# Gate logits with the tokens stationary, affinity transposes moved into the next image, and two weight splits moved to GpSimd

## The reference

```
x = x + attention(layernorm_c(x))          # 8 heads of 64, softmax over 1024 keys, fp32
t = tokens(x)
n = layernorm(t)
logits   = n @ gate_weight                 # 512 x 16 experts
affinity = softmax(logits).T               # [image, expert, token]
gating, index = top_k(affinity, 128)       # per image and expert
h = gelu(n[index] @ w1[e] + b1[e]);  y = h @ w2[e] + b2[e]
t = t + scatter_add(index, gating * y)
```

## Time and profile before

| what | value |
| --- | --- |
| median of three runs | 3219.74 us |
| profiled execution, its own time | 3216.83 us |
| span of the profiled execution | 3215.0 us |
| mean granted TensorE clock | 0.984 |
| PE busy | 3059.6 us (95%) |
| DVE busy | 2278.2 us (71%) |
| ACT busy | 1850.1 us (58%) |
| POOL busy | 1093.1 us (34%) |

### The profile page before, as it was taken

The page is one execution under the profiler, slowest core; times in us unless marked ns, Lnnn a source line. Parts: engine busy times, 40 slices in busy tenths (PEclk is TensorE's granted clock), DMA queues, the critical chain, the costliest instruction groups (busy, mean ns, idle before and its releaser), DMA issues. The chain is left out here.

```text
span 3215.0 us, 49747 instructions
## 1 busy us (share of the span) xinstructions
PE 3059.6 (95%) x18114; PEld 2627.4 (82%) x18114; DVE 2278.2 (71%) x3481; ACT 1850.1 (58%) x3353; POOL 1093.1 (34%) x1112
## 2 busy tenths in 40 slices
PE   6999999999999999999999999999917999999998
PEld 5988889888888888887988889888816788888886
DVE  5887688688768877876888688587775655655653
ACT  4876678477657857774876678477612333333332
POOL 1225224322512351252225124322513444444443
PEclk9999999999999999999999999999968999999999
DMA  7122121321321132113123121311224666666564
GB/s 236 37 60 106 64 63 50 112 67 37 105 88 50 50 115 77 37 57 118 58 60 109 61 63 57 105 41 37 63 96 94 135 141 133 135 143 137 129 144 59
DMA packets 121438, 283.59 MB, mean 88 GB/s; under 512 B 22417, under 2 KB 30609, under 8 KB 110481
## 3 DMA queue, kind: packets, MB, share of 16 engines
q1 hardware_dynamic: 92560, 213.72, 20.1%
q0 software_dynamic: 28672, 67.13, 11.8%
HBM read 173.08 MB, written 74.15 MB: 77 GB/s over the span
## 5 line engine op out<-in xcount | busy, mean ns | idle before, releaser
L754 DVE TENSOR_TENSOR PT<-ring,PT 128x512 fp32r<-128x512 f32 x1024 | 676.5, 686 | 160.4 <-ACT PT L503 142.2
L503 ACT ACTIVATE PT<-ring 128x512 fp32r<-128x512 f32 x1024 | 582.7, 597 | 169.8 <-PE ring L876 87.2
L908 PE MATMUL O<-PT,V 128*128 128x256 f32 x4096 | 673.0, 289 | 0.0
L696 DVE TENSOR_REDUCE nmax<-S 128x1 f32<-128x1024 f32 x512 | 619.8, 1211 | 71.7 <-PE S L865 71.7
L876 PE MATMUL ring<-ident,prob 128*128 128x128 f32 x4096 | 614.1, 273 | 15.3 <-DVE PT L754 12.9
L908 PEld LDWEIGHTS O<-PT,V 128*128 128x128 f32 x4096 | 575.4, 189 | 40.2
L865 PE MATMUL S<-kd,qs 128*128 128x512 f32 x2048 | 599.0, 414 | 2.7 <-ACT prob L494 1.7
L494 ACT ACTIVATE prob<-S,nmax 128x1024 f32<-128x1024 f32 x512 | 571.3, 1116 | 36.4 <-DVE nmax L696 36.4
L432 POOL COPY oS<-oHL 64x256 f32<-64x256 f32 x256 | 100.9, 394 | 1282.3 <-ACT oHL L552 1276.3
L876 PEld LDWEIGHTS ring<-ident,prob 128*128 128x128 f32 x4096 | 463.9, 139 | 55.3 <-issue 49.5
L865 PEld LDWEIGHTS S<-kd,qs 128*128 128x128 f32 x2048 | 347.2, 189 | 50.5 <-issue 6.0
(11 more groups left out here) (115 smaller groups left out, 3457.7 us busy)
## 6 DMA issues: line engine op xcount, KB each, us to landing
kd<-kd SPq DMA_DIRECT2D x128, 256.0 KB, 3.6
wraw<-w_dram SPq DMA_DIRECT2D x32, 1024.0 KB, 7.3
wqk<-wqk_split SPq DMA_DIRECT2D x24, 1024.0 KB, 4.8
xt<-x_dram SPq DMA_DIRECT2D x16, 1024.0 KB, 7.5
Rs<-rinv_rows SPq DMA_DIRECT2D x56, 256.0 KB, 3.4
PT<-wv_split SPq DMA_DIRECT2D x7, 2048.0 KB, 8.9
oT<-x_dram SPq DMA_DIRECT2D x24, 512.0 KB, 3.3
out_dram<-oT SPq DMA_DIRECT2D x48, 256.0 KB, 8.3
```

The lines of the kernel that those rows point to most:

```text
L503: nc.scalar.activation(PT[:, 0, u // 2 % 2, 4 * c:4 * c + 4, u % 2 * P:u % 2 * P + P], ring[:, k % 2, :].rearrange("p (m q) -> p m q", m=4 ...
L696: nc.vector.tensor_reduce(nmax[:, s:s + 1], S[:, s % 2, :], AX.X, ALU.max, negate=True).then_inc(max_done, 1)
L754: nc.vector.tensor_tensor(PT[:, 1, here[0], here[1], here[2]], ring[:, k % 2, :].rearrange("p (m q) -> p m q", m=4), PT[:, 0, here[0], her ...
L908: last_mm = nc.tensor.matmul(O[:, m % 2, 0:QC], V[:, t, head // 2, 2 * (head % 2):2 * (head % 2) + 2, :].rearrange("p h d -> p (h d)"), PT ...
```

## The change

It has two parts: the gate stage, and the start of the kernel.

Gate stage (PE, ACT and DVE lists):

```
# PE: the product, tokens stationary; one signal behind the eighth tile
-  last_mm = products(O[0:E, i // 4, i % 4 * P:i % 4 * P + P],
-                     [(gate_sb[:, c, :], n2T[:, i % 2, c, :]) for c in range(KC)])
-  if i % 4 == 3:
+  last_mm = products(O[:, 0, i * E:(i + 1) * E],
+                     [(n2T[:, i % 2, c, :], gate_sb[:, c, :]) for c in range(KC)])
+  if i == NT - 1:
       last_mm.then_inc(logits, 1)
# PE: the eight logit transposes and their wait go
-  pe.wait_ge(logits_copied, b * 2 + 2)
-  ... eight nc.tensor.transpose(O[:, 0, i * E:(i + 1) * E], affT[...], ident[0:E, 0:E])
# PE: affinity transposes, from ahead of scores(3) to between the halves of unit 1
+  def turn_affinities(j):
+      pe.wait_ge(soft, j * 5 + 5)
+      for h in range(2):
+          for i in range(4):
+              last_t = nc.tensor.transpose(O[0:E, 1 - h, i * P:(i + 1) * P], aff[:, 4 * h + i, :], ident)
+          last_t.then_inc(affT_filled, 1)
   # in turn_and_multiply
   turn_probs(b, u, c)
+  if u == 1 and c == 0 and b > 0:
+      turn_affinities(b - 1)
   # in product_with_v, part 0 of m == 0
+  if b > 0:
+      pe.wait_ge(affT_copied, b * 2)
# ACT: copy_logits (two activations an image) goes; the affinity copies move
   high_of_probs(b, s - 2)
+  if s == 3 and b > 0:
+      copy_affinities(b - 1)
# DVE: gate maximum and difference ahead of maximum(1), the rest behind it
   maximum(b + 1, 0)
-  maximum(b + 1, 1)
-  dve.wait_ge(logits_turned, b + 1)
+  dve.wait_ge(logits, b + 1)
   ... gmax, lg ...
+  if not last:
+      maximum(b + 1, 1)
   dve.wait_ge(soft_exp, b + 1)
   ... gsum, grec, aff ...
```

Start (POOL, ACT, DVE, SP lists):

```
# POOL, ahead of the low parts of V: the low parts of the V weights (0) and of split 2
+  for w in (0, 2):
+      pool.wait_ge(w_hi, w + 1)
+      raw, hi, lo, _ = splits[w]
+      nc.gpsimd.tensor_tensor(lo, raw, hi.bitcast(F32), ALU.subtract).then_inc(w_lo[w], 1)
# DVE keeps splits 1 and 3
-  if i in (3, 5, 7):
-      low_of_weights((i - 3) // 2)
+  if i == 5:
+      low_of_weights(1)
# ACT: the wait for the Q and K weights moves behind the second tile; casts behind tiles 1 and 2
-  act.wait_ge(wqk_raw_in, 32)
   for i in range(NT):
       high_of_norm(0, i)
-      if i in (1, 3):
-          high_of_weights(1 + i // 2)
+      if i in (1, 2):
+          act.wait_ge(wqk_raw_in, 32)
+          high_of_weights(i)
# ACT: the projected K waits for the K stage's stores alone, Q for the rest
-  act.wait_ge(w_out, 16 * 4 * (PAIRS - 1))
-  high_of_proj(0, 0)
+  act.wait_ge(w_out[0], 16 * 2 * (PAIRS - 1))
+  high_of_proj(0, 0, 0, 2)
+  act.wait_ge(w_out[1], 16 * (PAIRS - 1))
+  high_of_proj(0, 0, 2, 4)
# SP: each split is stored as soon as it is there; the load of Wo stands behind the first pair's stores
+  for j in range(2):
+      sp.wait_ge(w_lo[1 + j], 1)
+      for h in range(2):
+          store_split(0, j, h, w0_out)
   ... load Wo, wait w0_out, load_first_pair() ...
+  for j, h, n in ((0, 0, 0), (0, 1, 0), (1, 0, 1), (1, 1, 2)):
+      for p in range(1, PAIRS):
+          store_split(p, j, h, w_out[n])
```

More of the change, by code:

```diff
@@ L166, in attention @@
         w_hi = sem("w_hi")
-        w_lo = sem("w_lo")
+        w_lo = [sem(f"w_lo{w}") for w in range(4)]
         wv_out = sem("wv_out")
         w0_out = sem("w0_out")
-        w_out = sem("w_out")
+        w_out = [sem(f"w_out{i}") for i in range(3)]
         consts_in = sem("consts_in")
@@ L302, in _, with store_split @@
                 sp.dma_start(raw, wT[j]).then_inc(wqk_raw_in, 16)
-            sp.wait_ge(w_lo, 1)
+            sp.wait_ge(w_lo[0], 1)
             sp.dma_start(wv_dram, wv.bitcast(F32)).then_inc(wv_out, 16)
[L305 to L317, removed]
+            def store_split(p, j, h, done):
+                half = staged(j, h).bitcast(F32).rearrange("p (k c) -> p k c", k=KC)
+                sp.dma_start(wqk_dram[p, :, 2 * j + h, :, :], half[:, :, p * P:(p + 1) * P]).then_inc(done, 16)
+            for j in range(2):
+                sp.wait_ge(w_lo[1 + j], 1)
+                for h in range(2):
+                    store_split(0, j, h, w0_out)
+            raw = oT[:, 0:2, :].rearrange("p a n -> p (a n)").rearrange("p (k c) -> p k c", k=KC)
+            sp.dma_start(raw, wT[3]).then_inc(wo_raw_in, 16)
+            sp.wait_ge(w0_out, 16 * 4)
+            load_first_pair()
+            for j, h, n in ((0, 0, 0), (0, 1, 0), (1, 0, 1), (1, 1, 2)):
+                for p in range(1, PAIRS):
+                    store_split(p, j, h, w_out[n])
+            sp.wait_ge(w_out[2], 16 * (PAIRS - 1))
+            sp.wait_ge(w_out[1], 16 * (PAIRS - 1))
+            sp.wait_ge(w_out[0], 16 * 2 * (PAIRS - 1))
             load_pair(1)
@@ L510, in high_of_weights, with copy_affinities @@
                 nc.scalar.activation(hi, raw, ACT.Copy, scale=scale).then_inc(w_hi, 1)
+            def copy_affinities(j):
+                for i in range(2):
+                    act.wait_ge(affT_filled, j * 2 + i + 1)
+                    nc.scalar.activation(affT[:, 512 * i:512 * i + 512], O[0:E, 1 - i, :], ACT.Copy
+                                         ).then_inc(affT_copied, 1)
             act.wait_ge(ones_set, 1)
@@ L585, in image @@
                     high_of_proj(b + 1, 0, 0, 3)
[L587 to L590, removed]
                 for i in range(NT):
@@ L609, in image @@
                     high_of_probs(b + 1, 0)
[L610 to L613, removed]
+                if last:
+                    copy_affinities(b)
             all_images(act, image)
@@ L882, in _ @@
                 if i == 3:
-                    pe.wait_ge(w_lo, 1)
+                    pe.wait_ge(w_lo[0], 1)
                 if i >= 3:
@@ L893, in _ @@
             scores(0, 2)
-            pe.wait_ge(w_lo, 4)
+            pe.wait_ge(w_lo[3], 1)
             def image(b, last):
@@ L1028, in image @@
                     scores(b + 1, 1)
-                pe.wait_ge(logits_copied, b * 2 + 2)
-                pe.sem_inc(pe_passed, 1)
-                for i in range(NT):
-                    last_t = nc.tensor.transpose(O[:, 0, i * E:(i + 1) * E], affT[:, i * P:(i + 1) * P],
-                                                 ident[0:E, 0:E])
-                last_t.then_inc(logits_turned, 1)
                 if not last:
@@ L1038, in image @@
                     scores(b + 1, 2)
-                pe.wait_ge(soft, b * 5 + 5)
-                for h in range(2):
-                    for i in range(4):
-                        last_t = nc.tensor.transpose(O[0:E, 1 - h, i * P:(i + 1) * P], aff[:, 4 * h + i, :], ident)
-                    last_t.then_inc(affT_filled, 1)
+                if last:
+                    turn_affinities(b)
             all_images(pe, image)
```

7 lines of the change are left out of this document (1 added, 6 removed).

## The result

The changed kernel took 3205.59 us (median of five runs, 3203.38 to 3215.17), the kernel before 3219.74 us (five runs, 3217.6 to 3221.18): 0.9963 of the time, 95% interval 0.9947 to 0.9979. The forecast was 3224 us, so it had the wrong sign. The profiled execution took 3204.22 us, its span is 3202.4 us, against 3216.83 and 3215.0. The page gives PE, still the bound, 17 us less, and 64 instructions fewer. The weight loads have a row of their own, PEld, because they overlap the products.

A forecast was written before the change was run, and what follows sets the result against it. TensorE (PE), busy 95% of the span, was taken as the bound. Seven wraps +4.9, last image -0.9 and start +0.5 gave +4.5 us on the median of 3219.74: 3224 us, range 3196 to 3236.

The forecast's parts named there:

- The gate product: Gate stage on PE: 64 instructions an image at 0.116 instead of 0.109 us, 0.45 us an image lost.
- The argument from the 7 ns: Gate loads: 16 columns take 7 ns more than a transpose's, so a plain fp32 load makes two passes, 107 ns for 128.
- The first rival: Gate product: the load is one pass, 3.0 us saved an image instead of 0.45 lost, 3197 us; chance 0.13.
- From `scores(1)` to `scores(5)`: Wrap between images: exponential of unit 3, and `scores(5)` with it, 0.25 us late, seven times.
- the early gate exponential: Wrap, ScalarE: the exponential of unit 1 no longer waits behind the gate's and starts at 361.43, 0.68 us gained.
- the moved affinities: Wrap: affinity transposes between the halves of unit 1 leave ScalarE 0.65 us idle; the stop costs 0.93 us a wrap.
- The claim that `scores(1)` stays at 358.88: Wrap, PE: `scores(1)` keeps its time, and only the work behind it goes on some 1.1 us earlier.
- The last image: Gate stage of the last image: 1.35 us gained, 0.45 lost to the slower product, net -0.9 us.
- The 1.35 of copy and turn: Last image: copy, wait and transposes between ready logits and VectorE's start go, -1.35 us on the way to the barrier.
- The start: Start of the kernel: POOL's splits hold VectorE, projected K at 57.3, stores 1.4 us earlier; net +0.5 us.
- The base: Whole kernel: the median of 3219.74 us, to which the sum is added; the profiled execution stands 2.9 us under it.
- the likeliest case: Whole kernel: the forecast of 3224 us, its own range 3215 to 3233; chance 0.50.

The follow-up runs named there:

- e5: Kernel before, its stationary gate weights repeated to 128 columns once at the start, operand order, copies and transposes kept; 3209.16 us against 3219.01, one run.
- e10: Changed kernel with 128 streamed columns, affinity transposes and copies at their old place, and the split softmax undone; 3197.24 us, one run.
- e7: Changed kernel with 128 streamed columns and the affinity transposes and copies back at their old place; 3192.19 us (4 runs), 0.9918.
- e8: Changed kernel with 128 streamed columns and POOL's first split held back until three tiles are normalised; 3197.48 us, one run.
- e4: Changed kernel with 14 unused products on PE in the last image, ahead of the first gate product; 3207.46 us (7 runs), 0.9956.

## Why the prediction was wrong

**The gate product is the step that failed.** It was put as 64 instructions at 0.116 instead of 0.109 us, +0.45 us an image, and the stage measured 1.37 us less. The argument from the 7 ns was sound: the loads last 192 ns, two passes, as inferred, and follow at (0.97 - 0.192) / 7 = 0.111 us. By the Trainium skill (TensorE: Matmul & The Clock Gate, on LDWEIGHTS), which divides the columns by 1.2 GHz, it would be an estimated 0.107; the trace is 4% above that. What I never priced is what stands between the groups. I multiplied a pace by a count, read from merged rows that hold no gaps, and took the idle between the groups as given. The trace of before shows it in every tile, 0.21 and 0.17 us, and the row that groups the loads carries it as 12.4 us of idle ended by "issue". Five such periods an image, with the new pace already in them, went from 7.82 to 6.52 us (354.53 - 346.71 and 351.57 - 345.05), which is 1.30 of the 1.37 us. The entry and the end of the stage bring 0.6 more: 3.96 to 3.65 us from the first transposes to the first gate load, and `scores(1)` starts 0.08 us ahead of the end of the gate loads instead of 0.21 behind it. `e5` shows that these gaps belong to the narrow load. The first rival's 3197 lies nearer to the result than the forecast, but by luck: no load was one pass.

**From `scores(1)` to `scores(5)`** the forecast was +0.25 and +0.05 came. Its two halves hold: the early gate exponential was to bring 0.68 and `e10` against `e7` gives 0.73; the moved affinities were to take 0.93 and `e7` against the changed kernel gives 0.79. The claim that `scores(1)` stays at 358.88 fell with the gate product. A further 0.14 us a wrap (2.06 less 1.97 plus 0.05) lies somewhere in the rest of the image and was not looked for.

**The last image** was to bring 0.9 and lost 4.4. The 1.35 of copy and turn went as said. The failed step is that +0.45 us priced the product at the full clock: the stage ran at 1.2 GHz throughout and took 5.6 us more. The last stage of before had spent part of its time at the low clock too, and that was not in the forecast.

**The start** had every wait right and the sum wrong, by 1.85 us: that PE's clock stays at 1.00 behind a shorter hole was left out. The Trainium skill (SBUF — State Buffer, Who interferes with whom) has VectorE and GpSimd share a port that an instruction keeps to its end; the earlier trace rows agreed with it for 1.29 us, and 4.23 beside 4.50 and `e8` agree with it at 2048 elements.

**The sum.** The base was fair: the changed kernel's own profile lies 1.4 us under its median, that of before 2.9, so that 12.6 us of span stand for 14.15 between the medians. Against the forecast +4.5 the errors are -19.3 (wraps), +5.3 (last image), -1.85 (start) and -1.2 (experts), together -17.1, which gives the -12.6. The result lies in the lower half of the range, but the likeliest case had the wrong sign: it was the case with the finest arithmetic and a missing term.

## What to carry to other kernels

Before pricing an instruction by its pace, read the period of the whole repeated group, from one start to the next, and give each idle bracket a cause; an edit that changes an operand's shape may remove it. Where a 16-column stationary operand alternates with 128-column ones, widen it (by repeating it once, or by making the tokens stationary), and widen the streamed side too with a broadcast view: that cost 0.05 us a tile here, and no gate stage of images 0 to 6 lost its clock. The runs then lay within 3 to 6 us (four runs each) instead of 16 (ten). Test moves that come bundled with a gain one by one: of the two here one brought 0.73 us a wrap and the other took 0.79 back.

## What the runs showed of the hardware

- Eight-product groups with 128 loaded and 16 streamed columns fell to the 1.2 GHz level with PE and PEld both busy 3.00 of 3.00 us, from a granted clock of 1.00 just before (`e4`), in some images and not in others, 5 us a stage in image 2. What decides which image is caught stays open.
- A 16-column load among 128-column loads left the load queue idle 0.21 us ahead of the next group and 0.17 us ahead of its own; padded to 128 it left none.
- A POOL subtraction of 2048 elements took 4.50 us and held a VectorE product of eight elements, 0.17 us alone, for 4.23 us. A normalisation of 512 elements, 0.54 us alone, lasted 4.21 beside the second POOL subtraction.
- Behind a hole of 2.97 us in PE's work 24 products ran at a granted clock of 0.50 and took 7.13 us; behind one of 1.57 us they ran at 1.00 and took 5.76. Eight score products at 72 us took 3.47 us where the clock fell again and 2.09 where it didn't.
